# Two routed stages: logits and ranks earlier in TensorE's list, the shared expert's last chunk of tokens behind the expert blocks

## What is computed

```python
logits = jnp.einsum('bsd,de->bse', x, router_w)          # 8 columns
probs = jax.nn.softmax(logits, axis=-1)
top1_val, top1_idx = ...                                  # the largest of the 8
hid = jnp.einsum('bsd,edh->ebsh', x, up_w) * jax.nn.silu(jnp.einsum('bsd,edh->ebsh', x, gate_w))
mask = (top1_idx[None] == jnp.arange(Er)[:, None, None])  # Er = 7 routed experts
routed = jnp.einsum('ebsh,ehd,ebs->bsd', hid, down_w, mask)
shid = (x @ shared_up_w) * jax.nn.silu(x @ shared_gate_w) # hidden width 512
return 2.0 * top1_val[..., None] * routed + shid @ shared_down_w
```

## Time and profile before

| | us |
|---|---|
| runs | 1780.8, 1783.76, 1786.34 (median 1783.76) |
| profiled execution, its own time | 1781.01 |
| its span, first to last instruction | 1779.2 |
| mean granted TensorE clock | 0.951 |
| first routed stage | 123.9 to 259.3 |
| second routed stage | 566.6 to 695.7 |

### The profile page before, as it was taken

The page is one execution under the profiler, slowest core; times in us unless marked ns, Lnnn a source line. Parts: engine busy times, 40 slices in busy tenths (PEclk is TensorE's granted clock), DMA queues, the critical chain, the costliest instruction groups (busy, mean ns, idle before and its releaser), DMA issues. The chain is left out here.

```text
span 1779.2 us, 27350 instructions
## 1 busy us (share of the span) xinstructions
PE 1610.3 (91%) x9973; PEld 900.1 (51%) x10001; DVE 980.9 (55%) x2214; ACT 816.1 (46%) x1338; POOL 351.6 (20%) x492
## 2 busy tenths in 40 slices
PE   7889977999998997999699989998799978979998
PEld 2436654444444664446544555666434445545665
DVE  7673347888872434535554353446633457963444
ACT  5643323576765332432143333222698856743221
POOL 1314232232232422201330032001300100032000
PEclk9989988999998998999899999998899987989999
DMA  4642025110104201000000015553211024115553
GB/s 112 235 123 97 28 64 146 46 55 28 56 2 162 86 20 38 1 1 1 1 0 1 0 32 133 120 125 86 80 55 35 19 52 136 44 32 131 115 113 95
DMA packets 56231, 120.39 MB, mean 68 GB/s; under 512 B 8439, under 2 KB 35095, under 8 KB 51299
## 3 DMA queue, kind: packets, MB, share of 16 engines
q1 hardware_dynamic: 53628, 113.55, 23.4%
q0 software_dynamic: 2432, 5.00, 0.8%
q10 hardware_dynamic: 39, 0.07, 0.0%
HBM read 85.38 MB, written 19.96 MB: 59 GB/s over the span
## 5 line engine op out<-in xcount | busy, mean ns | idle before, releaser
L2479 DVE TENSOR_REDUCE a_most<-psum 128x1 f32<-128x512 f32 (+3 forms) x304 | 180.0, 653 | 42.7 <-PE psum L2325 31.7
L2437 ACT ACTIVATE a_probs<-psum 128x512 f32<-128x512 f32 (+1 forms) x304 | 153.0, 584 | 86.9 <-PE psum L2355 45.2
L3312 ACT ACTIVATE t_silu<-psum 128x512 f32<-128x512 f32 x136 | 81.2, 597 | 241.3 <-PE psum L3370 240.2
L3387 PEld LDWEIGHTS psum<-t_slot,t_hid 128*128 128x128 f32 x1024 | 132.1, 191 | 55.8 <-issue 49.7
L3483 DVE TENSOR_TENSOR t_prod<-t_silu,psum 128x512 f32<-128x512 f32 x104 | 71.5, 687 | 137.4 <-ACT t_silu L3312 137.4
L2740 ACT ACTIVATE ga_probs<-psum 128x1024 f32<-128x1024 f32 (+2 forms) x160 | 137.0, 952 | 19.6 <-PE psum L2109 18.9
L3387 PE MATMUL psum<-t_slot,t_hid 128*128 128x128 f32 x1024 | 134.4, 276 | 2.9 <-DVE t_hid L3474 2.9
L3370 PE MATMUL psum<-xnT,t_slot 128*128 128x512 f32 x256 | 131.5, 595 | 3.1 <-ACT t_silu L3312 3.1
L3375 PE MATMUL psum<-xnT,t_slot 128*128 128x512 f32 x256 | 130.7, 592 | 0.0
L2322 PE MATMUL psum<-a_ks,a_qs 96*128 96x512 bf16 (+3 forms) x384 | 119.3, 342 | 9.0 <-DVE a_most L2479 3.4
L3474 DVE TENSOR_TENSOR t_hid<-t_prod,t_spread 128x512 f32<-128x512 f32 x128 | 90.1, 707 | 38.3 <-DMA t_spread<-factors 31.8
(11 more groups left out here) (453 smaller groups left out, 3029.6 us busy)
## 6 DMA issues: line engine op xcount, KB each, us to landing
t_spread<-factors SPq DMA_DIRECT2D x64, 512.0 KB, 6.4
m_experts<-experts_dram SPq DMA_DIRECT2D x14, 768.0 KB, 9.1
c_halves<-xnT SPq DMA_DIRECT2D x48, 128.0 KB, 2.3
t_slot<-experts_dram SPq DMA_DIRECT2D x32, 192.0 KB, 5.2
a_qs<-scratch_q SPq DMA_DIRECT2D x16, 288.0 KB
a_ks<-scratch_k SPq DMA_DIRECT2D x24, 192.0 KB
ga_qs<-scratch_q SPq DMA_DIRECT2D x16, 288.0 KB
la_qs<-scratch_q SPq DMA_DIRECT2D x16, 288.0 KB
```

What stands on the lines that cost most here:

```text
L2437: act.activation(probs[:, (n * BLOCKS + b) % PROBS, h0:h0 + heads, 0:wide], src, ACT.Exp, scale=SCALE).then_inc(probs_ready, 1)
L2479: v.tensor_reduce(most[:, row, h0:h0 + heads, qt % KPH], src, AX.X, ALU.max).then_inc(max_read, 1)
L3312: act.activation(silu[:, n % 2, :], core.psum[:, g_bank(n), :], ACT.Silu).then_inc(silu_ready, 1)
L3387: ins = pe.matmul(core.psum[:, c, t * P:(t + 1) * P], left[:, t * P:(t + 1) * P], weights, start=pair < 0 and t == 0, stop=False, skip_gro ...
```

## The change

It reorders and changes no product. In TensorE's list logits(1) stands ahead of the first shared_up, logits(2) and (3) follow straight after the transposes, and the ranks come after shared_up(1) instead of shared_up(5). Only four products of the shared expert are early ones now (EARLY 6 to 4). ScalarE copies chunks 2 and 3 of xnT behind gate(0) with no gate between. The shared expert's last chunk (FRONT = 3) leaves its place ahead of the blocks: two of its shared_ups go into the last two rounds of the block loop, two and its shared_down behind the loop, with the matching silus and products on ScalarE and VectorE and the last shared_add ahead of the routed adds. SyncE waits for the last chunk's up products before it reads the routed results over that chunk of xnT.

```diff
--- before.py
+++ after.py
@@ -917,8 +917,9 @@
     H = HT * P
     GATE_AT, UP_AT, DOWN_AT = 0, H, 2 * H
     BLOCKS = (N + (E - 1) * (P - 1)) // P
-    SHARED, EARLY = NC * HT, 6
-    LATE = SHARED - EARLY
+    FRONT = NC - 1
+    SHARED, EARLY = FRONT * HT, 4
+    BEHIND = SHARED + BLOCKS
     GROUPS = [range(0, 2)] + [range(k, k + 4) for k in range(2, BLOCKS, 4)]
     group_of = {k: i for i, ks in enumerate(GROUPS) for k in ks}
     GATE, UP, DOWN, TURN, HIDT = (0, 1), (2, 3), (4, 5), 6, 7
@@ -995,6 +996,8 @@
                 sp.dma_start(rows[:, ks[0]:ks[-1] + 1, :], blocks_x[:, ks[0]:ks[-1] + 1, :]).then_inc(rows_in[i], 16)
             sp.wait_ge(returned, 16 * BLOCKS * (call + 1))
             for c in range(NC):
+                if c == FRONT:
+                    sp.wait_ge(up_pe, BEHIND + HT)
                 back = routed_y[1 + c * CH:1 + (c + 1) * CH, :].rearrange("(t p) d -> p t d", p=P)
                 sp.dma_start(core.routed[:, TPC * c:TPC * (c + 1), :], back).then_inc(core.routed_in[c], 16)
 
@@ -1015,7 +1018,7 @@
                     g.wait_ge(scattered, 16 * (NT * call + NT // 2))
             for k in range(BLOCKS):
                 g.wait_ge(token_ready, group_of[k] + 1)
-                g.wait_ge(out_read, NC + k + 1)
+                g.wait_ge(out_read, FRONT + k + 1)
                 to = bass.IndirectOffsetOnAxis(ap=token[:, k:k + 1], axis=0)
                 g.indirect_dma_start(routed_y, to, outs[:, k, :], None).then_inc(returned, 16)
 
@@ -1032,7 +1035,7 @@
 
             def turned_hid(k):
                 if k >= 2:
-                    act.wait_ge(down_pe, NC + k - 1)
+                    act.wait_ge(down_pe, FRONT + k - 1)
                 act.wait_ge(hidT_pe, k + 1)
                 act.activation(block_hidT[:, k % 2, :], core.psum[:, HIDT, :], ACT.Copy).then_inc(hidT_ready, 1)
 
@@ -1040,9 +1043,8 @@
             ln.scalar(act, 1)
             gate(0)
             ln.scalar(act, 2)
-            gate(1)
             ln.scalar(act, 3)
-            for n in range(2, EARLY):
+            for n in range(1, EARLY):
                 gate(n)
             act.wait_ge(shifted, 1)
             act.activation(prob[:, :, :], logit[:, :, :], ACT.Exp).then_inc(exps, 1)
@@ -1052,7 +1054,10 @@
             for k in range(1, BLOCKS):
                 gate(SHARED + k)
                 turned_hid(k - 1)
+            gate(BEHIND)
             turned_hid(BLOCKS - 1)
+            for j in range(1, HT):
+                gate(BEHIND + j)
             if last_work is not None:
                 last_work(act)
 
@@ -1074,7 +1079,7 @@
                 pe.matmul(core.psum[:, RANKS, P:2 * P], core.c("ones"), picks, start=True, stop=True).then_inc(ranks_pe, 1)
 
             def shared_up(n):
-                c, j = divmod(n, HT)
+                c, j = divmod(n if n < SHARED else n - BLOCKS, HT)
                 xc = core.xnT[:, c * CH:(c + 1) * CH]
                 if n == 0:
                     pe.wait_ge(shared_in, 16)
@@ -1091,12 +1096,13 @@
                 if c * HT < EARLY:
                     pe.wait_ge(early_ready, min(EARLY, (c + 1) * HT))
                 if (c + 1) * HT > EARLY:
-                    hid_done(pe, (c + 1) * HT - 1)
-                if c >= 2:
-                    pe.wait_ge(out_read, c - 1)
+                    hid_done(pe, (c + 1) * HT - 1 if c < FRONT else BEHIND + HT - 1)
+                nth = c if c < FRONT else FRONT + BLOCKS
+                if nth >= 2:
+                    pe.wait_ge(out_read, nth - 1)
                 for t in range(TPC):
                     for j in range(HT):
-                        ins = pe.matmul(core.psum[:, DOWN[c % 2], t * P:(t + 1) * P], hid[:, c % 2, j, t * P:(t + 1) * P],
+                        ins = pe.matmul(core.psum[:, DOWN[nth % 2], t * P:(t + 1) * P], hid[:, c % 2, j, t * P:(t + 1) * P],
                                         shared[:, DOWN_AT + j * P:DOWN_AT + (j + 1) * P], start=(j == 0), stop=(j == HT - 1))
                 ins.then_inc(down_pe, 1)
 
@@ -1126,35 +1132,30 @@
 
             def down(k, e):
                 pe.wait_ge(hidT_ready, k + 1)
-                pe.wait_ge(out_read, k + NC - 1)
+                pe.wait_ge(out_read, FRONT + k - 1)
                 for j in range(HT):
-                    ins = pe.matmul(core.psum[:, DOWN[k % 2], 0:D], block_hidT[:, k % 2, j * P:(j + 1) * P], weights(e, DOWN_AT + j * P, D),
+                    ins = pe.matmul(core.psum[:, DOWN[(FRONT + k) % 2], 0:D], block_hidT[:, k % 2, j * P:(j + 1) * P], weights(e, DOWN_AT + j * P, D),
                                     start=(j == 0), stop=(j == HT - 1))
                 ins.then_inc(down_pe, 1)
 
             ln.tensor(pe, 0)
             ln.tensor(pe, 1)
             logits(0)
+            logits(1)
             shared_up(0)
             ln.tensor(pe, 2)
-            logits(1)
-            shared_up(1)
             ln.tensor(pe, 3)
             logits(2)
             logits(3)
-            for n in range(2, EARLY):
-                shared_up(n)
+            shared_up(1)
             ranks()
-            for n in range(EARLY, 2 * HT):
+            for n in range(2, 2 * HT):
                 shared_up(n)
             shared_down(0)
-            for n in range(2 * HT, 3 * HT):
+            for n in range(2 * HT, SHARED):
                 shared_up(n)
             shared_down(1)
-            for n in range(3 * HT, SHARED):
-                shared_up(n)
             shared_down(2)
-            shared_down(3)
             pe.wait_ge(table_ready, 1)
             pe.wait_ge(experts_in, 16 * (E - 1))
 
@@ -1170,10 +1171,15 @@
                     gate_up(k, expert[k])
                     if k + 1 < BLOCKS:
                         expert[k + 1] = owner_of(k + 1)
+                else:
+                    shared_up(BEHIND + k - BLOCKS)
                 if 1 <= k <= BLOCKS:
                     turn_hid(k - 1)
                 if k >= 2:
                     down(k - 2, expert.pop(k - 2))
+            for j in range(2, HT):
+                shared_up(BEHIND + j)
+            shared_down(FRONT)
 
         @block.vector
         def _(v):
@@ -1233,9 +1239,10 @@
                 v.tensor_tensor(dst, silu[:, n % 2, :], core.psum[:, UP[n % 2], :], ALU.mult).then_inc(hid_ready, 1)
 
             def shared_add(c):
-                v.wait_ge(down_pe, c + 1)
+                nth = c if c < FRONT else FRONT + BLOCKS
+                v.wait_ge(down_pe, nth + 1)
                 xs = core.x[:, TPC * c:TPC * (c + 1), :].rearrange("p t d -> p (t d)")
-                v.scalar_tensor_tensor(xs, core.psum[:, DOWN[c % 2], :], 0.5, xs, ALU.mult, ALU.add).then_inc(out_read, 1)
+                v.scalar_tensor_tensor(xs, core.psum[:, DOWN[nth % 2], :], 0.5, xs, ALU.mult, ALU.add).then_inc(out_read, 1)
 
             def numbers(i):
                 ks = GROUPS[i]
@@ -1257,8 +1264,8 @@
                 multiply(n, hid[:, c % 2, j, :])
                 if c >= 2 and j == HT - 1:
                     shared_add(c - 2)
+            shared_add(1)
             shared_add(2)
-            shared_add(3)
             turned(0)
             for k in range(BLOCKS + 2):
                 if k + 1 < BLOCKS:
@@ -1269,11 +1276,18 @@
                     if k >= 2:
                         v.wait_ge(hidT_pe, k - 1)
                     multiply(SHARED + k, block_hid[:, k % 2, :])
+                else:
+                    multiply(BEHIND + k - BLOCKS, hid[:, FRONT % 2, k - BLOCKS, :])
                 if k >= 2:
-                    v.wait_ge(down_pe, NC + k - 1)
-                    v.tensor_copy(outs[:, k - 2, :], core.psum[:, DOWN[k % 2], 0:D]).then_inc(out_read, 1)
+                    v.wait_ge(down_pe, FRONT + k - 1)
+                    v.tensor_copy(outs[:, k - 2, :], core.psum[:, DOWN[(FRONT + k) % 2], 0:D]).then_inc(out_read, 1)
+            for j in range(2, HT):
+                multiply(BEHIND + j, hid[:, FRONT % 2, j, :])
+            shared_add(FRONT)
             for c in range(0 if later else NC):
                 v.wait_ge(core.routed_in[c], 16 * (call + 1))
+                if c == FRONT:
+                    v.wait_ge(out_read, FRONT + BLOCKS + 1)
                 for t in range(TPC * c, TPC * (c + 1)):
                     xs = core.x[:, t, :]
                     v.scalar_tensor_tensor(xs, core.routed[:, t, :], core.coef[:, t:t + 1], xs, ALU.mult, ALU.add)
```

## The result

| | before | after |
|---|---|---|
| median of the timed runs, us | 1785.45 (20 runs) | 1790.83 (20 runs) |
| lowest to highest, us | 1780.8 to 1790.11 | 1786.6 to 1794.65 |
| profiled execution: time / span, us | 1781.01 / 1779.2 | 1786.6 / 1784.6 |
| mean granted clock of TensorE (1 is 2.4 GHz) | 0.951 | 0.953 |

The changed kernel is slower: its ratio to the kernel before is **1.0031, 95% interval 1.0022 to 1.0040**, some 5.4 us. The forecast was +4.5 us, or 1788.3 on the median of three runs that was known then.

What follows compares the result with a forecast made beforehand. TensorE, busy 1610.3 of 1779.2 us, was taken as the bound, with two chains meeting at the blocks. Terms -0.6 + 3.4 + 1.7 = +4.5 us gave 1785.5 from the profiled execution, 1788.3 on the median; range 1779 to 1794.

Steps and rivals of the forecast that it cites:

- The ranks: Front of each routed stage: ranks run 6.15 us earlier in the first stage, 6.1 in the second, before the clock's share.
- The clock in front: Front: clock rises 1.73 us later, losing 0.87 us per stage, +1.7 in all (bounds 0 and 3.4).
- The chain behind the ranks: DVE and POOL, ranks to first scatter: scatter 4.5 us earlier, bounds 5.8 and 4.0, since POOL's multiplies hold up DVE.
- The wait before the blocks: Ahead of turn(0), the first block's first transpose: PE newly waits 2.8 us for rows, from 167.8 to 170.6.
- The blocks: Block loop: two moved shared_ups in the last two rounds make the last copy out 3.1 us later.
- the clock behind the wait: Start of the blocks: 3.4 us at half clock after the new wait, losing 1.7 us per stage, +3.4 in all.
- The tail: After T, the last copy out: routed adds wait for the shared add; 2.1 us later in stage 1, 3.2 in stage 2.
- The sum: Whole kernel: -0.6 us without the clock, +3.4 behind the wait, +1.7 in front, total +4.5; chance 0.45.
- signs that the prediction had named for being wrong: No wait or full clock before the blocks, scatter before 144, or next stage over 3 us earlier or later.
- the longer low stretch: Rival, start of the blocks: 6.8 us at half clock, losing 3.4 per stage; +7.9, 1791.7 us; chance 0.27.
- the held clock: Rival: clock holds at the blocks and rises in front where it rose before; -0.6, 1783.2 us; chance 0.17.
- rows in time for PE: Rival, start of the blocks: rows there when PE is, no new wait or half clock; -6.0, 1777.8 us; chance 0.11.

Runs made afterwards that it cites:

- e2: Kernel before with only the back of the change: chunk 3 moved behind the blocks, old front, six early products; 1799.09 us, ratio 1.0084.
- e5: Kernel before with ranks behind shared_up(3), shared_down(0) behind shared_up(5), EARLY 4, only shared_down(3) and its add behind the blocks; 1780.18 us, ratio 0.9972.
- e5 again: The unaltered e5 kernel measured once more, in five rounds; 1777.01 us, ratio 0.9959 to the kernel before.
- e10: Kernel before with only shared_down(3) and its add moved behind the blocks, ranks and logits where they were; 1785.19 us, ratio 1.0005.
- after twice: The changed kernel and its unaltered repeat, one profile each; 1790.83 us, ratio 1.0031, and 1789.33 us, ratio 1.0024.
- e1: Kernel before with only the new front: early logits and ranks, four early products, chunk 3 in its old place; 1791.18 us, ratio 1.0037.
- e3: Changed kernel with all shared_ups ahead of the blocks, only shared_down(3) and its add behind them; 1785.06 us, ratio 1.0007 to before.
- e8: Changed kernel with stage 1's routed adds of chunks 0 to 2 ahead of the last shared add; 1787.10 us, ratio 1.0013 to before.
- e6: Changed kernel with POOL waiting for its scatters to land after every four instead of once after eight; one run, 1797.73 us.
- e9: Changed kernel with the first scatter of a stage waiting until shared_down(0) has posted; one run, 1808.82 us.
- e4: Changed kernel with two early multiplies on POOL instead of four (EARLY 2); 1784.43 us, ratio 0.9996 to before.
- e7: Changed kernel with logits(1) behind shared_up(0), as in the kernel before; 1789.45 us, ratio 1.0027 to before.

## Why the prediction was right, point by point

**The ranks.** Expected 6.15 us earlier from the first logits, less 0.87 for the clock, so 5.3. Measured (stage 1 and stage 2) 5.9 and 3.7 in the first profile, 5.0 and 4.7 in the second. The 3.7 is the clock: in the second stage it rose at 575.0 and fell again, from 578.5 to 581.9, which kept shared_up(1) at half. Windows of the changed kernel:

```profile
174.00:177.40 3.40, 3.40 (x14) 1.85 (x13) 1.37 (x3) 1.32 (x3) 0.00 (x0) 1.00 0.66 180
578.50:581.90 3.40, 3.40 (x5) 1.33 (x5) 1.53 (x5) 0.60 (x1) 0.00 (x0) 0.50 0.83 339
616.00:619.40 3.40, 3.17 (x5) 1.59 (x6) 0.58 (x4) 0.60 (x1) 0.00 (x0) 0.50 1.08 289
```

**The clock in front, +0.87 a stage.** Counted from the first logits to its last rise in the front, the clock was low for 7.8 us in the mean of ten stages with the old order (before, e2, e5, e5 again, e10) and for 9.5 us in the mean of ten with the new one (after twice, e1, e3, e8). 1.7 us at half are 0.85 us. e6 and e9 have the new order too and bring its mean to 9.7; e4 is left out, since its clock falls once more behind the wait for hid. The step was right in the mean, and its bounds of 0 and 1.7 a stage were not too wide: single stages run from 4.5 to 11.4.

**The chain behind the ranks.** I took the scatter at 4.5 us earlier, with 4.0 as the bound if one more operation is held up. With the ranks at 5.9 it was 4.0: from the end of the ranks to the scatter 7.12 us instead of 5.38, so 1.74 longer where the sum had 1.65. Of the three operations named, L1209 took 0.86 us (1.06 before, as L1203), L1219 and L1221 1.18 and 1.35 instead of 0.29: -0.2 + 0.9 + 1.05 is the 1.74. e4 shows the last two at 0.29 when POOL is still. The other stages fell shorter: counted from the first logits, the scatter came 4.0 and 1.9 us earlier in the first profile and 3.4 and 2.9 in the second, where 4.5 less the clock's 0.87 is 3.6. In the second stage of the first profile it is the late ranks, by the clock.

By the rule of the Trainium skill (SBUF — State Buffer, Who interferes with whom) a DVE instruction with two SBUF inputs contends with a GpSimd instruction that reads SBUF, and the loser blocks fully. The traces agree for DVE: L1219 and L1221 took 1.18 and 1.35 us in the first profile instead of 0.29. In the second profile, first stage, three steps in a row met one multiply of POOL, each in another way:

```profile
143.09 0.29 DVE L1219 TENSOR_TENSOR m_taken<-m_ends,m_taken 128x128 f32<-128x128 f32 x1
143.22 1.29 POOL L1010 TENSOR_TENSOR m_hid<-m_silu,m_upper 128x512 f32<-128x512 f32 x1 [1.47 <-ACT m_upper L1034]
143.41 0.29 DVE L1220 TENSOR_TENSOR m_taken<-psum,m_taken 128x128 f32<-128x128 f32 x1
143.74 0.92 DVE L1221 TENSOR_TENSOR m_taken<-m_taken,m_chosen 128x128 f32<-128x128 f32 x1
```

L1219 began 0.13 us ahead of the multiply and was not held, L1220, with one input in PSUM, ran beside it and was not held, and L1221, with both in SBUF, ended 0.15 us behind it. The multiply itself, which began second to L1219, took 1.29 us instead of 1.26, so a full block of POOL doesn't show there. From the ranks' end to the scatter it took 6.55 us there, not 7.12. In the first profile, the scatter that the prediction put at 145.5 by it came at 146.69, in a stage that began 0.67 later: another 0.5 beyond, 0.3 of which were there at the ranks.

**The wait before the blocks, 2.8 us.** 2.48 and 3.02 us in the second profile, 2.7 to 3.1 in e7 and e8. In the first it was 0.55 and 2.03: in stage 1 PE came to it 1.3 us later than in the second, counted from the first logits, after one more wait for a silu (0.85) and 1.4 us more for the last two shared_downs, and the rows 0.6 earlier.

**The blocks, +3.1 us, and the clock behind the wait, +1.7.** At a full clock +2.9, which is the 3.1 less the quarter of a microsecond that DVE's earlier copy of turn(0) gives. With a low stretch of 3.4 us, +4.1: the stretch costs **1.2 to 1.5 us, not 1.7** (75.5 and 75.7 against 74.25; 72.62 against 71.36 in e10), and e7's 6.8 us cost 2.5. PE isn't without small waits there, which slower work can fill; no run shows that this is the reason. The clock didn't fall everywhere: in stage 1 of both profiles of the changed kernel it held, behind 0.55 and even behind 2.48 us of waiting; in stage 2 it fell for 3.4 us in both, in e7 and e8 in both stages. This term, +3.4 for both stages, was over-sized by 2.1: it came to 1.3 in each trace.

**The tail, +2.1 and +3.2.** +1.88 and +3.22; the shared add from T + 8.1, the end of the routed adds at T + 13.0 against T + 13.2, the next stage at T + 9.8. SyncE read back from T + 3.3 as the prediction had it, though the row of before that it goes by says T + 3.5 (250.78 against 247.32).

**The sum.** Predicted -0.6 + 3.4 + 1.7 = +4.5. The same pieces in the traces give +5.0 and +3.8, the medians 5.4 and 4.8. That it came so close is in part luck, for two misses cancel. The fronts were to be 9.4 us shorter with the clock's share, and were 7.1 and 8.3 (the scatters gained less); the blocks were to cost 8.7 and cost 7.0 in both (the clock behind the wait); the tails were to cost 5.3 and cost 5.1.

Two of the signs that the prediction had named for being wrong did appear. Stage 1 went through the start of the blocks at full clock in both profiles. And the stage behind the second routed stage started 5.1 and 3.3 us later than before, counted from the first logits, beyond the 3 that it allowed; its own terms for that stage, with the clock, make 2.6. The mechanism (a wait for rows, a longer end, moved work that isn't free) is what the traces show; the clock behind the wait came in one stage of two.

Of the rivals, the longer low stretch showed up in neither profile of the changed kernel, but in stage 1 of e7 and e10 and in both stages of e2, e6 and e9, the held clock in one stage of two, and rows in time for PE only in e4 among the kernels that move all of chunk 3, behind a wait of 2.0 us for hid. What was left open between the forecast and its rivals was of the size of a single low stretch.

## What to carry to other kernels

When two chains meet, one engine's list and a chain through the others, write down by how much a change shortens each, because only the smaller of the two is won: here the list lost 10.5 us of work and the other chain 2 to 4, and PE waited for part of the difference; the rest went into the slower front. Work that is moved behind a stage to fill an idle time is free only up to what that idle time was waiting for, so move the one product that fits there, not the whole chunk. Look at which engine works on the shared buffers while another runs a chain of small steps that everything waits for: two multiplies beside it made the chain 1.74 us longer in one stage and 1.17 in another, up to a whole shared_up.

## What the runs showed of the hardware that I had not expected

- The time from the last matmul to its signal was 3.3 to 3.7 us for shared_down(0) and (1) in the first profile of the changed kernel and those of e1 and e3, 7.6 once in e2, up to 1.5 in the kernel before, and 0.02 at most in a second profile of the same changed kernel. A single trace can hold a delay that is not the kernel's.
- The granted clock rose in a front and fell again 3.4 us later although PE had been idle for no more than 0.30 us (575.0 to 578.5 us in the changed kernel), with narrow logits and 128-column transposes in between.
- A low stretch of the clock of 3.4 us cost 1.2 to 1.5 us in the blocks, not half of its length.
- DVE's operation on 128x8 numbers, 0.17 us alone, waits for POOL's whole multiply: 0.65 to 1.07 us, and it ended no more than 0.03 us behind it in both stages of all fourteen traces.
- An operation on two SBUF tensors (128x128) that began 0.13 us ahead of POOL's multiply took its usual 0.29 us; those that began behind one took 0.92 to 1.36 in all traces where the two met.
